# Three partial products for r in the steps of a two-layer token mixer, and its first score mask moved to other engines

## The chip, the cores and the metric

One core of one Trainium2 chip runs the whole kernel. TensorE (PE) multiplies, VectorE (DVE), ScalarE (ACT) and GpSimd (POOL) do the element-wise work, and SyncE (SP) issues the loads and stores. The metric is the device time of one execution in microseconds, taken over several executions.

## The reference

The input x is 4 sequences of 1024 tokens with 256 channels, float32. Two residual layers follow each other.

```python
# layer 1, on a = layernorm(x)
q = a @ Wq + bq
k = (a @ Wk + bk) @ Wc @ We          # 64 columns: 4 heads of 16
v = (a @ Wv + bv) @ Wc @ We
qf, kf = elu(q) + 1, elu(k) + 1      # 16 query heads share 4 key heads
o = (qf . cumsum(kf v)) / (qf . cumsum(kf) + 1e-6)
x = x + layernorm(a + o @ Wo + bo) * gamma + beta
# layer 2, on z = layernorm(x)
xr = mu_r * z + (1 - mu_r) * z_prev  # z_prev: the token before
xk = mu_k * z + (1 - mu_k) * z_prev
r = sigmoid(xr @ W_r.T)
out = x + r * (square(relu(xk @ W_k.T)) @ W_v.T)
```

## The kernel before

The tokens are worked in 8 chunks of 128 tokens, all 4 sequences (batches b) at once, so a chunk is a tile of 128x1024. `step(c)` of each engine runs for c = 0 to 6 and then `finale(7)`. The order of every engine's work is written out by hand in its `step`; semaphores tie the engines together, and each engine does its own list strictly in order.

Step c works on three chunks at once: n = c+1 (its queries, keys and values), c (its attention), m = c-1 (output projection, residual, first layernorm) and f = c-2 (the second layer, called the FFN here). Steps 2 to 6 have an FFN (f >= 0); these five are the repeating part. The FFN of the last three chunks is in the finale.

What the change touches, with the lines of the profile:

- Scores. PE writes the scores of one batch into the four banks `ps_z` (L471). DVE's `mask(c, b)` multiplies them with `causal` into `probs[b % 2]` (L1086), and PE's `outputs(c, b)` (L487, L492) reads these. `mask(c, 0)` is the first thing in DVE's step. PE's `spread_reciprocals` (L454) writes `ps_z` again and so waits for that mask; ACT copies its result out as `rden_bc`.
- Second layer. PE transposes z (`transpose_z`, L508), ACT copies it to `zT` (`shift_z`), after moving one column (128x8) as carry. POOL's `token_difference` makes `dz` in two halves (L290). DVE's `token_shift` (L1145) makes `xr` (two halves, early in the step) and `xk` (two halves, later), each from `dz` and `zT`. PE's `mix_r` (L522) multiplies xr with W_r in float32, 8 products of 128x256, each issued as two matmuls. `mix_k` (L515) and `mix_v_parts` (L553, L557) follow.
- Products in parts. For the queries and for v, ACT copies a float32 tile to type fp32r (the high part), DVE subtracts to get the low part, and PE makes three products: high x high, high x low, low x high. `low_a` (L1203) and `low_part` (L1209) are the DVE sides. `mix_r_parts` (L532, L536) does this for r in the finale, for the last chunk only.
- Norms. POOL's `first_norm(m)` (L225, L227) turns the variance of y into `rstd1`, which DVE's `second_residual` (`x2_tok`, listed as x_tok, L1130) needs. `norm_x(n+1)` does it for x. POOL's `add_bo` (`abo_tok`, L267) and `add_beta` (`xb_tok`, L274) are 128x1024 adds, `denominator_terms` (`prod`, L282) a 128x1024 product.
- Key features. ACT makes exp(k) (L801), DVE clips it at 1 (L1041) and makes kf (L1044). DVE's `centre` (y_tok, L1119) lies between `keys_values` (L1036, L1037) and that.
- Each list waits where it must; DVE's list in an FFN step is: mask 0, norm_x, xr (2), add_residual 0 and 1 with their statistics, mask 1, keys_values, centre (4), key_features, low_a (2), second_residual (4), divide 0, mask 2, queries 0, xk (2), queries 1, divide 1, states, key_sums, second_stats, mask 3, divide 2, low_part (2), reciprocal, divide 3, gate (2).

Of the kernel before, what the change touches and what calls it, by code (L numbers as in the profile page):

```python
# [7 lines left out]
P = 128  # L8
# [10 lines left out]
def build(nc, x, wq, bq, wk, bk, wv, bv, wc, we, wo, bo, gamma, beta, w_r, w_k, w_v, mu_r, mu_k, out):  # L19
# [14 lines left out]
    with ExitStack() as ctx:  # L34
# [16 lines left out]
        def view(t, start, *shape):  # L51
# [41 lines left out]
        prod = sb("prod", 2, T)  # L93
# [13 lines left out]
        xr_p, wr_split, s_xrh, s_xrl = aT_p, sem("wr_split"), sem("xr_high"), sem("xr_low")  # L107
        s_aTh, s_aTl, wq_split = sem("aT_high"), sem("aT_low"), sem("wq_split")
        s_kah, s_kal, wv_split = sem("kact_high"), sem("kact_low"), sem("wv_split")
        y_tok, z_tok = sb("y_tok", NB, D), sb("z_tok", NB, D)  # L110
# [24 lines left out]
        s_kv_ps, s_kv, s_ek, s_ekm, s_kf, s_vh, s_vp = (  # L135
            sem("kv_ps"), sem("kv_ready"), sem("expk"), sem("expk_min"), sem("kf_ready"), sem("v_half_ready"), sem("v_heads_ready"))
# [10 lines left out]
        s_vl, s_gl = sem("last_v_ps"), sem("last_gated")  # L147
        s_last, s_den = sem("last_out_ready"), sem("den_ready")
# [21 lines left out]
            16 * len(part) for part in (kv_loads, c_loads, bias_loads, q_loads, ffn_loads, row_loads))  # L170
        ka_value = lambda m: 2 * m + 2 if m < LAST else 2 * (LAST - 2) + 2
# [43 lines left out]
        def _(pool):  # L215
# [83 lines left out]

            def step(c):  # L300
                n, m, f = c + 1, c - 1, c - 2
                if f >= 0:
                    token_difference(f)
                if n + 1 < NC:
                    norm_x(n + 1)
                if f >= 0:
                    add_bo(n)
                    first_norm(m)
# [79 lines left out]
        def _(pe):  # L388
# [137 lines left out]
            def mix_r_parts(i, bk_):  # L526
                pe.wait_ge(s_xrh, 2)
                for b in (2 * i, 2 * i + 1):
# [4 lines left out]
                    if b == 0:  # L533
                        pe.wait_ge(s_xrl, 2)
# [44 lines left out]
            def step(c):  # L579
# [90 lines left out]
            def finale(c):  # L670
# [114 lines left out]
        def _(act):  # L785
# [11 lines left out]
            def keys(n):  # L797
# [3 lines left out]
                AC.activation(ek[:], kb[:], ACT.Exp).then_inc(s_ek, 1)  # L801
# [89 lines left out]

            def gate_r(m, i, bk_):
# [4 lines left out]

            def step(c):
                n, m, f = c + 1, c - 1, c - 2
                if f >= 0:  # L900
                    shift_z(f, x0, x1)
# [9 lines left out]
                if f >= 0:  # L911
                    for k in range(KD):
# [35 lines left out]
            def finale(c):  # L948
# [60 lines left out]
        def _(dve):  # L1009
# [151 lines left out]
            def step(c):  # L1161
                n, m, f = c + 1, c - 1, c - 2
                mask(c, 0)
# [9 lines left out]
                add_residual(m, 0, x1)  # L1173
                add_residual(m, 1, x2)
# [62 lines left out]
            def finale(c):  # L1237
# [34 lines left out]
                for k in range(KD):  # L1272
                    dve.wait_ge(s_xrh, k + 1)
                    V.tensor_tensor(xr_p[1][:, k, :], xr[:, k].rearrange("p b t -> p (b t)"), xr_p[0][:, k, :].bitcast(F32),
                                    ALU.subtract).then_inc(s_xrl, 1)
# [78 lines left out]
```

## Time and profile before

| | |
|---|---|
| median of 3 executions | 276.59 us (276.57 to 277.20) |
| the profiled execution | 276.82 us, span 275.1 us, so 1.7 us lie around the span |
| granted TensorE clock, mean | 0.984 |
| PE | 258.8 us busy, 94% |
| DVE | 229.4 us busy, 83% |
| ACT | 163.8 us busy, 60% |
| POOL | 143.9 us busy, 52% |

A line of the timeline has a start in us from the beginning of the span, a duration, the engine, the line of the kernel, out<-in, shapes and a count; neighbours of one kind are merged, so that the duration of "x2" covers both. Brackets hold the idle time before it and what ended it. POOL's busy time includes time in which it waits for memory.

### The profile page before, as it was taken

What the parts mean: (1) busy time and instruction counts of PE and PEld (TensorE: products, weight loads), DVE (VectorE), ACT (ScalarE), POOL (GpSimd) and SP (SyncE); (2) the same over time, 40 slices, a digit from 0 to 9 for tenths busy, and PEclk for the clock granted to TensorE, in tenths of its full rate; (3) what the DMA queues carried; (4) which work ended last, traced back from release to release, by engine and by line L of the source; (5) the groups of instructions that cost most, each with busy time, mean ns of one, the idle gap of its engine ahead of it and who ended that gap; (6) DMA issues with size and microseconds to landing.
All of it is one profiled execution on the core that took longest, in us unless ns stands there. A gap on an engine that the chain in (4) does not pass through costs nothing.

```text
span 275.1 us, 7641 instructions
## 1 busy us (share of the span) xinstructions
PE 258.8 (94%) x2997; PEld 193.6 (70%) x2997; DVE 229.4 (83%) x558; ACT 163.8 (60%) x329; POOL 143.9 (52%) x165
## 2 busy tenths in 40 slices
PE   7998989987999999999999999999999999997993
PEld 6856557745787588758886688758875777683863
DVE  6578576875999989898999989996999868999484
ACT  1458585675756965486737964686348830363680
POOL 2636494599653678335833686355533633055340
PEclk9799999997999999999999999999999999999998
DMA  5910220000200021000400020001000020000213
GB/s 156 287 61 1 79 77 6 4 0 2 76 4 2 0 93 64 1 4 13 142 2 2 2 76 4 1 4 47 32 2 4 2 76 2 2 0 0 77 38 118
DMA packets 12180, 10.75 MB, mean 39 GB/s; under 512 B 2288, under 2 KB 12144, under 8 KB 12144
## 3 DMA queue, kind: packets, MB, share of 16 engines
q1 hardware_dynamic: 11392, 9.97, 11.3%
q8 instruction: 24, 0.39, 0.6%
q10 hardware_dynamic: 752, 0.30, 0.4%
q14 instruction: 12, 0.10, 0.1%
HBM read 6.07 MB, written 4.19 MB: 37 GB/s over the span
## 4 chain that ended last, share of the span: by engine, by line
PE 57%; DVE 17%; issue 9%; ACT 7%; POOL 6%; DMA 2%; POOLq 1%; DVEq 0%; ACTq 0%
PE ps_x L500 9%; PE ps_x L515 7%; PE ps_x L522 6%; PE ps_x L404 4%; PE ps_z L471 4%; PE ps_y L487 4%; PE ps_y L492 4%; PE ps_x L553 4%; DVE xk L1145 4%; DVE stats L1014 2%; PE ps_z L731 2%; DMA out_dram<-out_tok 2%; PE ps_x L397 2%; PE ps_x L417 2%; PE ps_x L508 2%
## 5 line engine op out<-in xcount | busy, mean ns | idle before, releaser
L1086 DVE TENSOR_TENSOR probs<-ps_z,causal 128x1024 f32<-128x1024 f32 x32 | 38.7, 1208 | 1.0 <-PE ps_z L471 0.8
L274 POOL TENSOR_TENSOR xb_tok<-x_in,beta_bc 128x1024 f32<-128x1024 f32 x8 | 19.1, 2388 | 22.0 <-DVE x_tok L1130 22.0
L500 PE MATMUL ps_x<-wo_sb,oT 128*128 128x256 f32 x128 | 29.9, 382 | 0.0
L297 POOL TENSOR_TENSOR out_tok<-tanh_r,x_tok 128x512 f32<-128x512 f32 x14 | 18.3, 1313 | 20.9 <-DVE tanh_r L1158 20.9
L282 POOL TENSOR_TENSOR prod<-qf,ksum 128x1024 f32<-128x1024 f32 x7 | 16.5, 2359 | 22.3 <-DVE ksum L1059 22.3
L267 POOL TENSOR_TENSOR abo_tok<-a_tok,bo_bc 128x1024 f32<-128x1024 f32 x8 | 18.9, 2365 | 17.0 <-issue 6.8
L500 PEld LDWEIGHTS ps_x<-wo_sb,oT 128*128 128x128 f32 x128 | 23.5, 190 | 3.7 <-issue 0.5
L227 POOL TENSOR_TENSOR rstd<-rstd,neg_half 128x4 f32<-128x4 f32 x24 | 24.5, 1021 | 1.9
L487 PE MATMUL ps_y<-qf,state 32*32 32x128 f32 x512 | 20.9, 278 | 3.9 <-DVE oT L1098 3.4
L471 PE MATMUL ps_z<-qf,kfT 32*128 32x128 f32 x512 | 23.5, 298 | 0.9 <-DVE qf L1050 0.4
L487 PEld LDWEIGHTS ps_y<-qf,state 32*32 32x32 f32 x512 | 12.2, 105 | 16.0 <-issue 13.1
L471 PEld LDWEIGHTS ps_z<-qf,kfT 32*128 32x128 f32 x512 | 17.4, 187 | 6.9 <-issue 4.5
L492 PE MATMUL ps_y<-probs,v_pad 128*32 128x128 f32 x512 | 21.1, 283 | 0.0
L290 POOL TENSOR_TENSOR dz<-zT 128x512 f32<-128x512 f32 x14 | 14.7, 1073 | 8.2 <-ACT zT L789 8.2
L515 PE MATMUL ps_x<-xk,wkT 128*128 128x512 f32 x40 | 18.5, 605 | 0.4
L809 ACT ACTIVATE eq<-ps_x,neg_bq 128x512 f32<-128x512 f32 x15 | 10.3, 687 | 13.6 <-PE ps_x L420 12.8
L522 PE MATMUL ps_x<-wrT,xr 128*128 128x256 f32 x80 | 18.1, 379 | 0.0
L789 ACT ACTIVATE zT<-ps_x 128x512 f32<-128x512 f32 x16 | 8.7, 594 | 15.7 <-PE ps_x L508 15.7
L855 ACT ACTIVATE a_tok<-x_in,nbias,rstd 128x256 f32<-128x256 f32 x24 | 12.4, 589 | 8.8 <-issue 5.5
L869 ACT ACTIVATE z_tok<-x_tok,nbias,rstd 128x256 f32<-128x256 f32 x32 | 16.6, 594 | 0.6 <-POOL nbias L235 0.6
L1050 DVE SCALAR_TENSOR_TENSOR qf<-ps_x,bq,eq 128x512 f32<-128x512 f32 x15 | 11.2, 748 | 6.8 <-ACT eq L811 6.8
L492 PEld LDWEIGHTS ps_y<-probs,v_pad 128*32 128x32 f32 x512 | 12.2, 110 | 6.6 <-issue 6.1
(175 smaller groups left out, 663.4 us busy)
## 6 DMA issues: line engine op xcount, KB each, us to landing
x_in<-in_L_attn_x_dram SPq DMA_DIRECT2D x8, 512.0 KB, 4.3
out_dram<-out_tok SPq DMA_DIRECT2D x16, 256.0 KB, 2.1
xr<-in_L_attn_Wq_dram ACTq DMA_DIRECT2D x1, 256.0 KB, 4.2
xk<-in_L_ffn_W_r_dram SPq DMA_DIRECT2D x1, 256.0 KB, 5.5
xk<-in_L_ffn_W_k_dram SPq DMA_DIRECT2D x1, 256.0 KB, 5.7
xr<-in_L_ffn_W_v_dram SPq DMA_DIRECT2D x1, 256.0 KB, 6.3
wo_sb<-in_L_attn_Wo_dram SPq DMA_DIRECT2D x4, 64.0 KB, 4.6
bo_bc<-in_L_attn_bo_dram SPq DMA_DIRECT2D x1, 128.0 KB, 5.5
```

Source lines behind the costliest of these rows:

```text
L227: PL.tensor_tensor(dst[:], dst[:], neg_half[:], ALU.pow).then_inc(done, 1)
L267: PL.tensor_tensor(abo_tok[n % 2][:], a_tok[n % 2][:], bo_bc[:].unsqueeze(1).to_broadcast([P, NB, D]), ALU.add).then_inc(s_ab, 1)
L274: PL.tensor_tensor(xb_tok[n % 2][:], x_in[n % XBUF][:], beta_bc[:].unsqueeze(1).to_broadcast([P, NB, D]), ALU.add).then_inc(s_xb, 1)
L297: PL.tensor_tensor(out_tok[:, 2 * i:2 * i + 2, :], tanh_r[:, i].rearrange("p (b d) -> p b d", b=2), x2_tok[m % 3][:, 2 * i:2 * i + 2, :], ...
L471: last = mm(ps_z[:, g, u * P:(u + 1) * P], kfT[c % 2][rows, 2 * b + u, :, :], qf[c % 2][rows, :, t0:t0 + HALF], start=True, stop=True, ski ...
L487: mm(ps_y[rows, off + u * P:off + (u + 1) * P], state[rows, slot, b, :, :], qf[c % 2][rows, :, t0:t0 + HALF], start=(u == 0), stop=False, ...
L492: last = mm(ps_y[32 * g:32 * g + 32, off + u * P:off + (u + 1) * P], v_pad[c % 2][:, b, u, g, :, :], probs[b % 2][:, g, u * P:(u + 1) * P] ...
L500: last = mm(bk_[:, (b % 2) * D:(b % 2 + 1) * D], oT[m % 2][:, a, b, :], wo_sb[:, a, :], start=(a == 0), stop=(a == 1))
L515: last = mm(bk_[:, :], wkT[:, k, n * P:(n + 1) * P], xk[:, k, :, :], start=(k == 0), stop=(k == KD - 1))
L522: last = mm(bk_[:, (b % 2) * D:(b % 2 + 1) * D], xr[:, k, b, :], wrT[:, k, :], start=(k == 0), stop=(k == KD - 1))
L869: AC.activation(z_tok[:, b, :], x2_tok[m % 3][:, b, :], ACT.Identity, bias=nbias2[:, b:b + 1], scale=rstd2[:, b:b + 1]).then_inc(s_z, 1)
L1086: V.tensor_tensor(probs[b % 2][:].rearrange("p g (r s) -> p g r s", s=HALF), ps_z[:, :, 0:2 * P].rearrange("p g (r s) -> p g r s", s=HALF) ...
```

## The change

1. r of the FFN steps is made in three products of parts. ACT gets `high_xr(f)` (two copies of 128x512), DVE gets `low_xr(f)` (two subtractions of 128x512) between the two `add_residual`, PE runs `mix_r_parts` in place of `mix_r`. The parts of xr get tiles of their own; the space comes from `prod` (now the same tile as `eq`) and `z_tok` (now `a_tok`).
2. `mask(c, 0)` of the FFN steps leaves DVE. ACT copies the first scores to `probs[0]` (`first_scores`, ahead of `shift_z`), POOL multiplies them in place with `causal` (`mask_first`, between `token_difference` and `norm_x`), and `outputs(c, 0)` waits for POOL.
3. The clip of exp(k) leaves DVE: ACT computes relu(-k) and then exp of its negative, two instructions in place of one.
4. DVE's order becomes queries 0, xk 0, queries 1, xk 1.
5. POOL does `first_norm(m)` ahead of `add_bo(n)`.
6. Waits that go with the shared tiles: ACT's queries wait for the denominators of the chunk before, `normalise_z` for `add_bo`.

```diff
-        prod = sb("prod", 2, T)
+        prod = eq
...
-        xr_p, wr_split, s_xrh, s_xrl = aT_p, sem("wr_split"), sem("xr_high"), sem("xr_low")
+        xr_p = [ctx.enter_context(nc.sbuf_tensor(f"xr_{part}", [P, KD, T], F32R)) for part in ("high", "low")]
...
-        y_tok, z_tok = sb("y_tok", NB, D), sb("z_tok", NB, D)
+        y_tok, z_tok = sb("y_tok", NB, D), a_tok
...
+            def mask_first(c):
+                pool.wait_ge(s_pr, 8 * c + 2)
+                rows = probs[0][:].rearrange("p g (r s) -> p g r s", s=HALF)
+                PL.tensor_tensor(rows, rows, causal[:].unsqueeze(1).unsqueeze(1).to_broadcast([P, G, 4, HALF]),
+                                 ALU.mult).then_inc(s_first, 1)
...
                 if f >= 0:
                     token_difference(f)
+                if f >= 0:
+                    mask_first(c)
                 if n + 1 < NC:
                     norm_x(n + 1)
                 if f >= 0:
+                    first_norm(m)
                     add_bo(n)
-                    first_norm(m)
                     add_beta(n)
...
             def outputs(c, b):
+                if b == 0 and 2 <= c < LAST:
+                    pe.wait_ge(s_first, c - 1)
...
                     pe.wait_ge(s_y, 2 * m + 1)
-                    mix_r(f, 0, x1)
+                    pe.wait_ge(wr_split, 2)
+                    mix_r_parts(f, 0, x1)
                     pe.wait_ge(s_y, 2 * m + 2)
-                    mix_r(f, 1, x2)
+                    mix_r_parts(f, 1, x2)
...
-                AC.activation(ek[:], kb[:], ACT.Exp).then_inc(s_ek, 1)
+                AC.activation(ek[:], kb[:], ACT.Relu, scale=-1.0).then_inc(s_nk, 1)
+                act.wait_ge(s_nk, n + 1)
+                AC.activation(ek[:], ek[:], ACT.Exp, scale=-1.0).then_inc(s_ek, 1)
...
+            def high_xr(m):
+                if m >= 1:
+                    act.wait_ge(s_r_ps, 2 * m)
+                for k in range(KD):
+                    act.wait_ge(s_xr, 2 * m + k + 1)
+                    copy(xr_p[0][:, k, :], xr[:, k].rearrange("p b t -> p (b t)")).then_inc(s_xrh, 1)
...
+            def first_scores(c):
+                act.wait_ge(s_sc, 8 * c + 2)
+                act.wait_ge(s_o, 4 * c - 1)
+                copy(probs[0][:], ps_z[:, :, 0:2 * P]).then_inc(s_pr, 2)
+
             def step(c):
                 n, m, f = c + 1, c - 1, c - 2
                 if f >= 0:
+                    first_scores(c)
                     shift_z(f, x0, x1)
...
                 if f >= 0:
+                    high_xr(f)
                     for k in range(KD):
                         act.wait_ge(s_aT, 2 * n + k + 1)
...
             def key_features(n):
                 dve.wait_ge(s_ek, n + 1)
-                V.tensor_scalar(ek[:], ek[:], 1.0, None, ALU.min).then_inc(s_ekm, 1)
-                dve.wait_ge(s_ekm, n + 1)
...
-                mask(c, 0)
+                if f < 0:
+                    mask(c, 0)
...
                 add_residual(m, 0, x1)
+                low_xr(f)
                 add_residual(m, 1, x2)
...
                 queries(n, 0, x0)
                 token_shift(f, 0, *for_k)
+                queries(n, 1, x1)
                 token_shift(f, 1, *for_k)
-                queries(n, 1, x1)
...
+            def low_xr(m):
+                if m >= 1:
+                    dve.wait_ge(s_r_ps, 2 * m)
+                for k in range(KD):
+                    dve.wait_ge(s_xrh, xr_value(m) - 1 + k)
+                    V.tensor_tensor(xr_p[1][:, k, :], xr[:, k].rearrange("p b t -> p (b t)"), xr_p[0][:, k, :].bitcast(F32),
+                                    ALU.subtract).then_inc(s_xrl, 1)
```

## Rows read from the trace of the kernel before

**Rows 1.** Busy time of each engine in one whole FFN step (step 4).

```profile
core 0: us, PE busy (x) PEld busy (x) DVE busy (x) ACT busy (x) POOL busy (x), PEclk, DMA share, GB/s
128.73:159.00 30.27, 30.07 (x370) 22.81 (x369) 28.04 (x68) 20.43 (x41) 17.43 (x18) 1.00 0.12 36
```

**Rows 2.** Timeline of PE in the same step.

```profile
138.18 3.62 PE L522 MATMUL ps_x<-wrT,xr 128*128 128x256 f32 x16
...
155.93 0.39 PE L553 MATMUL ps_x<-wv_high,ka_high 128*128 128x256 f32 x1
...
159.00 0.73 PE L471 MATMUL ps_z<-qf,kfT 32*128 32x128 f32 x16
```

**Rows 3.** Timeline of DVE in the same step.

```profile
132.52 1.87 DVE L1145 SCALAR_TENSOR_TENSOR xr<-dz,mu_r_col,zT 128x512 f32<-128x512 f32 x2
...
137.55 1.19 DVE L1086 TENSOR_TENSOR probs<-ps_z,causal 128x1024 f32<-128x1024 f32 x1
...
139.32 1.66 DVE L1119 SCALAR_TENSOR_TENSOR y_tok<-y_tok,mv,gamma_bc 128x256 f32<-128x256 f32 x4
140.90 0.29 DVE L1041 TENSOR_SCALAR ek<-ek 128x256 f32<-128x256 f32 x1
141.30 0.43 DVE L1044 SCALAR_TENSOR_TENSOR kf<-kb,ek 128x256 f32<-128x256 f32 x1
141.65 1.28 DVE L1203 TENSOR_TENSOR aT_low<-aT,aT_high 128x512 fp32r<-128x512 f32 x2
...
144.76 1.22 DVE L1086 TENSOR_TENSOR probs<-ps_z,causal 128x1024 f32<-128x1024 f32 x1
146.61 0.75 DVE L1050 SCALAR_TENSOR_TENSOR qf<-ps_x,bq,eq 128x512 f32<-128x512 f32 x1 [0.63 <-ACT eq L811]
...
153.00 1.19 DVE L1086 TENSOR_TENSOR probs<-ps_z,causal 128x1024 f32<-128x1024 f32 x1
154.31 0.42 DVE L1098 TENSOR_TENSOR oT<-ps_y,rden_bc 128x256 f32<-128x256 f32 x1
```

**Rows 4.** Timeline of ACT in the same step.

```profile
130.47 1.09 ACT L789 ACTIVATE zT<-ps_x 128x512 f32<-128x512 f32 x2 [2.36 <-PE ps_x L508]
...
131.92 1.04 ACT L789 ACTIVATE rden_bc<-ps_z 128x1024 f32<-128x1024 f32 x1
...
158.17 0.21 ACT L789 ACTIVATE zT<-zT 128x8 f32<-128x8 f32 x1
```

**Rows 5.** Timeline of POOL in the same step.

```profile
131.14 2.04 POOL L290 TENSOR_TENSOR dz<-zT 128x512 f32<-128x512 f32 x2 [0.18 <-ACT zT L789]
...
136.57 2.37 POOL L267 TENSOR_TENSOR abo_tok<-a_tok,bo_bc 128x1024 f32<-128x1024 f32 x1 [0.74 <-ACT a_tok L855]
138.90 0.20 POOL L225 TENSOR_TENSOR rstd<-mv,ln_eps 128x4 f32<-128x4 f32 x1
139.18 1.02 POOL L227 TENSOR_TENSOR rstd<-rstd,neg_half 128x4 f32<-128x4 f32 x1
144.59 2.41 POOL L274 TENSOR_TENSOR xb_tok<-x_in,beta_bc 128x1024 f32<-128x1024 f32 x1 [4.39 <-DVE x_tok L1130]
```

**Rows 6.** Timeline of DVE and POOL at two moments of the finale, one instruction a line.

```profile
246.32 0.48 DVE L1130 SCALAR_TENSOR_TENSOR x_tok<-y_tok,rstd,xb_tok 128x256 f32<-128x256 f32 x1
246.40 1.30 POOL L290 TENSOR_TENSOR dz<-zT 128x512 f32<-128x512 f32 x1 [1.11 <-ACT zT L789]
...
246.72 1.26 DVE L1130 SCALAR_TENSOR_TENSOR x_tok<-y_tok,rstd,xb_tok 128x256 f32<-128x256 f32 x1
...
247.66 1.22 POOL L290 TENSOR_TENSOR dz<-zT 128x512 f32<-128x512 f32 x1
247.90 1.52 DVE L1145 SCALAR_TENSOR_TENSOR xk<-dz,mu_k_col,zT 128x512 f32<-128x512 f32 x1
```

**Rows 7.** Busy time and granted clock in two stretches of step 1.

```profile
61.20:64.60 3.40, 1.21 (x32) 0.78 (x32) 3.31 (x8) 2.56 (x7) 3.24 (x6) 1.00 0.00 0
64.60:68.10 3.50, 3.44 (x56) 2.61 (x60) 0.40 (x2) 1.83 (x5) 3.50 (x2) 0.51 0.02 5
```

More of the change, by code:

```diff
@@ L106, in build @@
         wr_p = [ctx.enter_context(nc.sbuf_tensor(f"wr_{part}", [P, KD, D], F32R)) for part in ("high", "low")]
-        xr_p, wr_split, s_xrh, s_xrl = aT_p, sem("wr_split"), sem("xr_high"), sem("xr_low")
+        xr_p = [ctx.enter_context(nc.sbuf_tensor(f"xr_{part}", [P, KD, T], F32R)) for part in ("high", "low")]
+        wr_split, s_xrh, s_xrl = sem("wr_split"), sem("xr_high"), sem("xr_low")
         s_aTh, s_aTl, wq_split = sem("aT_high"), sem("aT_low"), sem("wq_split")
         s_kah, s_kal, wv_split = sem("kact_high"), sem("kact_low"), sem("wv_split")
-        y_tok, z_tok = sb("y_tok", NB, D), sb("z_tok", NB, D)
+        y_tok, z_tok = sb("y_tok", NB, D), a_tok
         stats1, mv1, rstd1 = sb("stats1", NB, 6), sb("mv1", NB, 2), sb("rstd1", NB)
@@ L134, in build @@
             sem("aT_ps"), sem("aT_ready"), sem("q_ps"), sem("negq"), sem("expq"), sem("qf_ready"))
-        s_kv_ps, s_kv, s_ek, s_ekm, s_kf, s_vh, s_vp = (
-            sem("kv_ps"), sem("kv_ready"), sem("expk"), sem("expk_min"), sem("kf_ready"), sem("v_half_ready"), sem("v_heads_ready"))
+        s_kv_ps, s_kv, s_ek, s_nk, s_kf, s_vh, s_vp = (
+            sem("kv_ps"), sem("kv_ready"), sem("expk"), sem("negk"), sem("kf_ready"), sem("v_half_ready"), sem("v_heads_ready"))
         s_kT_ps, s_kT, s_ks, s_dS_ps, s_tail, s_state = (
@@ L147, in build @@
         s_vl, s_gl = sem("last_v_ps"), sem("last_gated")
+        s_first = sem("first_probs_masked")
         s_last, s_den = sem("last_out_ready"), sem("den_ready")
@@ L170, in build @@
             16 * len(part) for part in (kv_loads, c_loads, bias_loads, q_loads, ffn_loads, row_loads))
+        xr_value = lambda m: 2 * m + 2 if m < LAST else 2 * (LAST - 2) + 2
         ka_value = lambda m: 2 * m + 2 if m < LAST else 2 * (LAST - 2) + 2
@@ L507, in transpose_z @@
                     for k, bk_ in ((0, bk0), (1, bk1)):
-                        last = tr(bk_[:, b * P:(b + 1) * P], z_tok[:, b, k * P:(k + 1) * P], ident[:])
+                        last = tr(bk_[:, b * P:(b + 1) * P], z_tok[m % 2][:, b, k * P:(k + 1) * P], ident[:])
                         if b == NB - 1:
@@ L524, in mix_r, with mix_r_parts @@
                 last.then_inc(s_r_ps, 1)
-            def mix_r_parts(i, bk_):
-                pe.wait_ge(s_xrh, 2)
+            def mix_r_parts(m, i, bk_):
+                pe.wait_ge(s_xrh, xr_value(m))
                 for b in (2 * i, 2 * i + 1):
@@ L533, in mix_r_parts @@
                     if b == 0:
-                        pe.wait_ge(s_xrl, 2)
+                        pe.wait_ge(s_xrl, xr_value(m))
                     for k in range(KD):
@@ L720, in finale @@
                 pe.wait_ge(wr_split, 2)
-                mix_r_parts(0, z2)
+                mix_r_parts(c, 0, z2)
                 pe.wait_ge(s_th, 2 * m + 2)
-                mix_r_parts(1, z3)
+                mix_r_parts(c, 1, z3)
                 pe.wait_ge(s_gt, 2 * m + 1)
@@ L808, in queries @@
                     act.wait_ge(s_qf, 2 * n - 1 + a)
+                    act.wait_ge(s_den_ps, n)
                 AC.activation(eq[:, a, :], bk_[:, :], ACT.Relu, bias=neg_bq[:, a:a + 1], scale=-1.0).then_inc(s_nq, 1)
@@ L865, in normalise_z @@
                 act.wait_ge(s_nb2, 2 * m + 2)
+                act.wait_ge(s_ab, min(m + 3, NC))
                 if m >= 1:
@@ L868, in normalise_z @@
                 for b in range(NB):
-                    AC.activation(z_tok[:, b, :], x2_tok[m % 3][:, b, :], ACT.Identity, bias=nbias2[:, b:b + 1],
+                    AC.activation(z_tok[m % 2][:, b, :], x2_tok[m % 3][:, b, :], ACT.Identity, bias=nbias2[:, b:b + 1],
                                   scale=rstd2[:, b:b + 1]).then_inc(s_z, 1)
@@ L963, in finale @@
                 gate_r(m, 1, z3)
-                for k in range(KD):
-                    act.wait_ge(s_xr, 2 * c + k + 1)
-                    copy(xr_p[0][:, k, :], xr[:, k].rearrange("p b t -> p (b t)")).then_inc(s_xrh, 1)
+                high_xr(c)
                 channel_k(c, 0, z0, True)
@@ L1271, in finale @@
                 token_shift(c, 1, *for_r)
[L1272 to L1275, printed above, removed]
+                low_xr(c)
                 gate(m, 0, x1)
```

## The prediction

> **What bounds it now.** I read the page's busy shares first, then the chain that ended last, then cut the span into steps. The chain repeats five times with a period of 30.27 us, and most of it is PE; in one such step PE is busy for 30.07 of 30.27 us at full clock, and DVE for 28.04 [rows 1]. So PE sets the pace, but DVE is nearly full and has almost no air. To see how much, I followed DVE's list through one step. It waits in only two kinds of place. One is 0.63 us ahead of queries 0, for ACT's exponential [rows 3]. The other is where PE has to deliver: divide 2 starts at 154.31, while a mask that starts at 153.00 leaves DVE free about 1.14 us later (144.76 plus 1.22, less the 0.08 by which neighbours overlap), at 154.14, so 0.17 us of slack; and the two gates at the step's end, which wait for mix_v and are PE's business. Between xr at the front and divide 2 the list therefore has 0.8 us of air, and divide 2 releases PE's last outputs, mix_v and with them the next step. Whatever lengthens DVE by more than 0.8 us in that stretch lengthens the step.
>
> I call T the start of the scores that open a step, 128.73 here (159.00 less the period) [rows 1, 2].
>
> **What decides: who blocks whom.** In the finale DVE runs four x_tok in a row, each 0.48 us. POOL's dz is issued at 246.40, while the third runs. The fourth, issued at 246.72, takes 1.26 us in place of 0.48 and ends at 247.98, 0.28 behind dz's end at 247.70; dz itself takes 1.30 [rows 6], of which 1.02 is its own time by the pair of 2.04 [rows 5]. Then xk, issued at 247.90 under the second dz (which ends at 248.88), takes 1.52 and ends 0.54 behind it [rows 6]. So a POOL instruction and a DVE instruction of two SBUF inputs exclude each other for their whole length, and a waiting POOL instruction gets in between two DVE instructions that stand back to back. The masks, which read PSUM, are not stretched: 1.19 with abo_tok running over it, 1.22 with xb_tok [rows 3, 5]. In the step the same is seen at xr: two halves take 1.87 us, since the first waits for the second dz [rows 3, 5].
>
> The Trainium skill (SBUF — State Buffer, section "SBUF: two separate sides") states this as a rule: VectorE and GpSimd share one pair of ports, a VectorE instruction with two SBUF inputs and a GpSimd one that reads SBUF take it as an exclusive lock for the whole instruction, and the other "fully blocks". By that rule the sum is the one below; were the two to share the ports in parts, or not at all, it would be the fourth case. The trace agrees, by the 1.26 and 1.52 us above.
>
> **The change part by part**, on DVE's path from zT to divide 2, in us per FFN step.
>
> 1. First scores on ACT. They end at about T+0.73 [rows 2]. The copy is bound by rden_bc, the same shape out of the same banks: 1.04 us; the carry column (0.21, now done ahead of the step in idle time) comes behind it [rows 4]. zT then starts at T+1.95 in place of T+1.74 (130.47) [rows 4]. That is +0.21 for dz. DVE itself is freed of 1.14 us ahead of norm_x, and this is worth nothing: DVE then stands waiting for dz, which hangs on PE's transposes and ACT.
> 2. mask_first on POOL. Its price is that of abo_tok, 128x1024 with a broadcast, 2.37 us; xb_tok at 2.41 bounds it above and the two dz halves at 2.04 below [rows 5]. It is issued when the second dz ends, while xr 0 has been waiting for the ports; xr 0 goes first, as now; mask_first waits and goes in between, as dz did between the x_tok; xr 1 is blocked. It begins some 0.12 ahead of xr 0's end (246.80 against 247.70 less 1.02 [rows 6]), and xr 1 ends 0.54 behind it in place of 0.66 behind xr 0: 2.37 - 0.12 + 0.54 - 0.66 = +2.13. The wait that outputs 0 gets for it costs nothing: the mask ends near T+7.5, outputs 0 comes after T+13.
> 3. low_xr on DVE, the same as aT_low: 1.28 less 0.08 overlap [rows 3], +1.20. Its high parts are ready: ACT needs about 0.55 us behind each xr (half of zT's 1.09 [rows 4]), and add_residual 0 with its statistics stands between.
> 4. first_norm ahead of add_bo. Today abo_tok runs from 136.57 to 138.94, under statistics, mask 1 and keys_values, and ends before centre at 139.32 [rows 3, 5]. In the new order POOL waits for the statistics of y, which end where mask 1 starts (call it 0), does L225 and L227 (0.07 + 0.28 + 1.02, less 0.04) and begins abo_tok at 1.33, until 3.70. Centre is issued at 139.32 - 137.55 = 1.77 and has two SBUF inputs. Its first instruction ends at 3.98 and not at 2.25: +1.73. The other order would have avoided this only if POOL were free early, which mask_first and the norm of x behind it prevent.
> 5. The clip goes: 140.90 to 141.30 [rows 3], -0.40. ACT's second instruction on the keys (kf of the same size takes 0.43 on DVE, so about 0.45) is covered by centre's 1.66 [rows 3].
> 6. k's shifts. xb_tok starts behind x_tok, 0.17 ahead of mask 2, and ends at 147.00. Without the 0.63 us of air, queries 0 would start at 145.90 and xk 0 at 146.57; it waits until 147.00 and ends 0.54 later, 147.54 in place of 147.31 [rows 3, 5]: +0.23. That queries 1 comes one shift earlier lets mix_k start some 0.66 earlier against DVE, but the end of the stretch is divide 2, and DVE's sum up to there is unchanged: 0.
> 7. r in parts. mix_r takes 3.62 less overlap, 3.54; the same count of products in parts takes 155.93 to 159.00, 3.07 [rows 2]. PE is shorter by 0.47, and this is worth nothing here, since PE will wait for DVE.
> 8. ACT gets 1.04 + 1.09 + 0.45 = 2.6 us on 20.4 of 30.27 [rows 1, 4]: covered. The waits for the shared tiles look at work of the step before: 0. Steps 0 and 1 and the finale change by a tenth at most.
>
> **Sum:** 0.21 + 2.13 + 1.20 + 1.73 - 0.40 + 0.23 = 5.10; less the air, 0.63 and 0.17: **+4.30 us a step**, a period of 34.6 us. Five steps: +21.5. Against the profiled execution (276.82, which is 0.23 above the median of the runs) that gives **298.3 us**. With mask_first between 2.04 and 2.41 it is 296.7 to 298.5.
>
> **Rivals.**
>
> - *The clock falls.* Low_a ends near T+19.1 (141.65 + 1.28 is T+14.2 today [rows 3], and items 1 to 5 add 4.87), and PE, with its high products done, would be there near T+16: a wait of about 3 us. In step 1 PE was busy for 1.21 of 3.40 us and the granted clock was then 0.51, the lower of the two levels (1.2 GHz in place of 2.4), for 3.5 us [rows 7]. Such a fall costs up to half of 3.5 us, of which part lies in the wait. From 0 to 1.75 a step, I take 0.8: 302.3 us. For it: the wait is longer than any in an FFN step now. Against it: before and behind it PE is dense. Chance 0.15.
> - *xr 1 gets the ports ahead of mask_first.* Then mask_first runs from the end of xr 1, and low_xr, issued 1.4 us later, waits about 0.85 for it. In place of 2.13 the step pays 0.85: +3.0 a step, 291.9 us. Against it stands x_tok and dz. Chance 0.12.
> - *Only one of the two large blocks happens*, since abo_tok or mask_first comes at another time than I place it: 4.30 - 1.73 = 2.57 or 4.30 - 2.13 = 2.17 a step, 289.7 or 287.7 us. Chance 0.10.
> - *The blocks do not count*, as if the ports were free: 0.21 + 1.20 - 0.40 - 0.80 = +0.21, or nothing at all if xr 1 runs unblocked. 276.6 to 277.9 us. Chance 0.06.
> - *Faster.* DVE's list is a little shorter by count (1.14 and 0.40 go, 1.20 comes), and PE loses 0.47 us. If the step stays PE's, as it is by the shares, all of that shows: 5 x 0.47 = 2.4 us, 274.4 us. Its place is mix_r on PE; it decides if what DVE gets up to divide 2 stays under its 0.8 us of air, so if mask_first and abo_tok both fall under instructions that read PSUM. Chance 0.07.
>
> The forecast has 0.50. The range is 287 to 304: it takes in the first three rivals and leaves out the last two with 0.13 and the tails. A measurement of this kernel tells apart about 0.3%, 0.8 us. Slower by over that has 0.50 + 0.15 + 0.12 + 0.10 and part of the fourth, 0.89; within it 0.04; faster 0.07.
>
> **What will show it.** In an FFN step of the new profile: one of the two xr takes near 3 us with mask_first over it; the first centre takes about 2.2 us in place of 0.48, with abo_tok over it; PE is idle for several us, ended by DVE's aT_low and xr_low; the period is about 34.6 us; mix_r_parts takes 3.1 us. I am wrong if mask_first and xr run over each other unstretched, if the centre instructions stay at 0.48, or if PE stays busy for 29.5 us of a shorter step.

## The result and the profile after

The changed kernel takes 300.75 us (median of 4, 299.32 to 302.62) beside 276.89 us for the kernel before (median of 4, 276.57 to 277.54): a ratio of 1.0876, 95% interval 1.0839 to 1.0914. The forecast was 298.3 us, range 287 to 304. The profiled execution took 300.64 us, its span 298.9.

The page of the changed kernel, parts 1 and 2, to be read against the table of the kernel before:

```profile
PE 263.8 (88%) x3037; PEld 196.0 (66%) x3037; DVE 249.0 (83%) x555; ACT 177.6 (59%) x352; POOL 156.4 (52%) x170
...
PEclk9999999979999999799998999779997999999999
```

PE fell from 94% to 88% of a longer span, and DVE's busy time rose by 19.6 us although three fewer instructions run on it: its instructions are longer, not more. The clock row shows four dips in the repeating steps that were not there before (at 122, 156, 191 and 228 us); the one near 65 us, in step 1, is in both pages.

Three FFN steps of the changed kernel, busy time by engine (columns as in [rows 1]):

```profile
101.78:136.91 35.13, 31.37 (x381) 23.46 (x380) 32.03 (x68) 22.99 (x45) 19.91 (x19) 0.95 0.11 32
136.91:172.07 35.16, 31.43 (x380) 23.71 (x380) 32.13 (x68) 23.00 (x45) 20.07 (x19) 0.95 0.10 31
172.07:208.43 36.36, 32.60 (x380) 24.42 (x380) 32.26 (x68) 22.99 (x45) 19.66 (x19) 0.91 0.05 16
```

The period was 30.27 us. DVE has 68 instructions in a step as before, and 32.1 us busy in place of 28.0. T, the start of the scores, is 136.84 for the second of these. DVE's timeline in that step:

```profile
140.69 4.20 DVE L1173 SCALAR_TENSOR_TENSOR xr<-dz,mu_r_col,zT 128x512 f32<-128x512 f32 x2 [1.25 <-POOL dz L293]
144.82 0.68 DVE L1137 TENSOR_TENSOR y_tok<-ps_x,abo_tok 128x512 f32<-128x512 f32 x1
...
146.20 1.28 DVE L1240 TENSOR_TENSOR xr_low<-xr,xr_high 128x512 fp32r<-128x512 f32 x2
...
149.20 1.19 DVE L1114 TENSOR_TENSOR probs<-ps_z,causal 128x1024 f32<-128x1024 f32 x1
...
150.97 3.50 DVE L1147 SCALAR_TENSOR_TENSOR y_tok<-y_tok,mv,gamma_bc 128x256 f32<-128x256 f32 x4
...
157.85 1.21 DVE L1114 TENSOR_TENSOR probs<-ps_z,causal 128x1024 f32<-128x1024 f32 x1
...
159.64 0.96 DVE L1173 SCALAR_TENSOR_TENSOR xk<-dz,mu_k_col,zT 128x512 f32<-128x512 f32 x1
160.99 0.75 DVE L1078 SCALAR_TENSOR_TENSOR qf<-ps_x,bq,eq 128x512 f32<-128x512 f32 x1 [0.40 <-ACT eq L828]
...
166.06 1.19 DVE L1114 TENSOR_TENSOR probs<-ps_z,causal 128x1024 f32<-128x1024 f32 x1
167.31 0.42 DVE L1126 TENSOR_TENSOR oT<-ps_y,rden_bc 128x256 f32<-128x256 f32 x1
```

and POOL's:

```profile
139.54 2.04 POOL L293 TENSOR_TENSOR dz<-zT 128x512 f32<-128x512 f32 x2 [0.46 <-ACT zT L803]
141.54 2.81 POOL L306 TENSOR_TENSOR probs<-probs,causal 128x1024 f32<-128x1024 f32 x1
...
150.62 2.38 POOL L270 TENSOR_TENSOR abo_tok<-a_tok,bo_bc 128x1024 f32<-128x1024 f32 x1
157.67 2.38 POOL L277 TENSOR_TENSOR xb_tok<-x_in,beta_bc 128x1024 f32<-128x1024 f32 x1 [4.67 <-DVE x_tok L1158]
```

Two of DVE's instructions by themselves, the second xr and the first centre:

```profile
142.05 2.84 DVE L1173 SCALAR_TENSOR_TENSOR xr<-dz,mu_r_col,zT 128x512 f32<-128x512 f32 x1
...
150.97 2.31 DVE L1147 SCALAR_TENSOR_TENSOR y_tok<-y_tok,mv,gamma_bc 128x256 f32<-128x256 f32 x1
```

The reader is to lay the two engines on each other. Mask_first is issued at 141.54, waits for xr 0, and takes 2.81 us, of which about 2.37 are its own (the price of abo_tok). The second xr is issued at 142.05 and ends at 144.89: 2.84 us in place of 0.74. Abo_tok starts at 150.62, 0.35 ahead of centre, whose four instructions then take 3.50 us in place of 1.66, all of the excess in the first (2.31). Xb_tok holds xk back by 0.2. Mask 2 at 157.85 reads PSUM; xb_tok runs over all of it, and it takes 1.21 us, as before (1.22). DVE is idle for 1.25 us ahead of xr, which is the place where mask 0 used to be.

PE waits for aT_low, and in four of the five FFN steps the clock falls behind the wait. PE's timeline of the step, and its busy time and clock before and behind:

```profile
156.05 0.96 PE L431 MATMUL ps_x<-aT_low,wq_high 128*128 128x512 f32 x2 [2.94 <-DVE aT_low L1233]
156.81 0.63 PE L428 MATMUL ps_x<-aT_high,wq_high 128*128 128x512 f32 x1
```

```profile
153.10:156.50 3.40, 0.46 (x3) 0.40 (x3) 3.40 (x9) 0.90 (x2) 0.00 (x0) 0.98 0.00 0
156.50:160.00 3.50, 3.50 (x24) 2.36 (x22) 3.50 (x7) 1.71 (x3) 2.33 (x1) 0.53 0.00 0
...
190.70:197.50 6.80, 6.27 (x43) 4.20 (x44) 6.14 (x11) 3.89 (x8) 2.39 (x1) 0.51 0.01 2
```

With 0.46 us of work in 3.40, the granted clock is then 0.53, the lower level (1.2 GHz), for 3.5 us; in the following step it stays there for 6.8 us, and that step is the one of 36.36 us. The first FFN step has the same wait and no fall:

```profile
86.41 0.50 PE L431 MATMUL ps_x<-aT_low,wq_high 128*128 128x512 f32 x1 [2.96 <-DVE aT_low L1233]
...
86.40:89.90 3.50, 3.49 (x43) 2.48 (x44) 3.50 (x7) 2.63 (x5) 1.88 (x1) 1.00 0.00 0
```

### The profile page after: what moved, and what is told of

Same layout as the page of the kernel before. It is cut to its first block, busy times and chain, and to the rows that moved or that the text cites. A ratio compares the mean times of both kernels' runs of the same rounds, so it can differ in the third digit from the quotient of the medians.

```text
span 298.9 us, 7762 instructions
## 1 busy us (share of the span) xinstructions
PE 263.8 (88%) x3037; PEld 196.0 (66%) x3037; DVE 249.0 (83%) x555; ACT 177.6 (59%) x352; POOL 156.4 (52%) x170
## 4 chain that ended last, share of the span: by engine, by line
PE 46%; DVE 33%; issue 9%; ACT 6%; POOL 4%; DVEq 0%; POOLq 0%; ACTq 0%
PE ps_x L513 5%; DVE xr L1173 5%; PE ps_x L528 5%; DVE stats L1044 4%; PE ps_y L500 4%; DVE y_tok L1147 4%; PE ps_y L505 4%; PE ps_x L566 4%; DVE probs L1114 3%; PE ps_z L482 3%; DVE y_tok L1137 3%; PE ps_x L431 2%; PE ps_x L521 2%; DVE aT_low L1233 2%; PE ps_x L428 2%
## 5 line engine op out<-in xcount | busy, mean ns | idle before, releaser
L1114 DVE TENSOR_TENSOR probs<-ps_z,causal 128x1024 f32<-128x1024 f32 x27 | 32.5, 1203 | 0.9 <-PE ps_z L482 0.8
L1173 DVE SCALAR_TENSOR_TENSOR xr<-dz,mu_r_col,zT 128x512 f32<-128x512 f32 x16 | 25.2, 1617 | 7.5 <-POOL dz L293 7.5
L285 POOL TENSOR_TENSOR eq<-qf,ksum 128x1024 f32<-128x1024 f32 x7 | 16.6, 2368 | 21.7 <-DVE ksum L1087 21.7
L500 PE MATMUL ps_y<-qf,state 32*32 32x128 f32 x512 | 22.0, 290 | 4.2 <-DVE oT L1126 3.8
L431 PE MATMUL ps_x<-aT_low,wq_high 128*128 128x512 f32 x20 | 9.3, 558 | 14.8 <-DVE aT_low L1233 14.8
L505 PE MATMUL ps_y<-probs,v_pad 128*32 128x128 f32 x512 | 21.9, 292 | 0.0
L1147 DVE SCALAR_TENSOR_TENSOR y_tok<-y_tok,mv,gamma_bc 128x256 f32<-128x256 f32 x28 | 20.9, 803 | 0.0
L887 ACT ACTIVATE a_tok<-x_tok,nbias,rstd 128x256 f32<-128x256 f32 x32 | 16.6, 592 | 0.7 <-POOL nbias L238 0.6
L415 PE MATMUL ps_x<-wkv_sb,aT 128*128 128x128 f32 x128 | 16.4, 282 | 0.5 <-ACT aT L803 0.5
L234 POOL TENSOR_TENSOR neg_mean<-mv,neg_one 128x4 f32<-128x4 f32 x17 | 5.6, 327 | 21.3 <-DVE mv L1050 21.2
```

The source lines that it names most:

```text
L1114: V.tensor_tensor(probs[b % 2][:].rearrange("p g (r s) -> p g r s", s=HALF), ps_z[:, :, 0:2 * P].rearrange("p g (r s) -> p g r s", s=HALF) ...
L1147: V.scalar_tensor_tensor(out=y_tok[:, b, :], in0=y_tok[:, b, :], scalar=mv1[:, b, 0:1], in1=gamma_bc[:], op0=ALU.subtract, op1=ALU.mult).t ...
L1173: V.scalar_tensor_tensor(out=dst[:, k], in0=dz[:, k], scalar=mu[:, k:k + 1], in1=zT[:, k, :, 0:P], op0=ALU.mult, op1=ALU.add).then_inc(don ...
```

## The experiments

All ratios are against the kernel before on the same chip. The medians in us come from more than one chip, so where two variants are compared the ratios are the safer pair. A step's period is read from the starts of the second gate (DVE tanh_r) in two successive steps, unless another row is shown.

**1. Is the clock fall a cost of its own?** The high products of queries 0 are issued three times more, in PE's wait.

```diff
             def query_parts(n, a, bk_):
                 pe.wait_ge(s_aTh, 2 * n - 4)
+                for again in range(3 if a == 0 else 0):
+                    for k in range(KD):
+                        for part in range(2):
+                            mm(bk_[:, :], wq_p[part][:, k, a, :], aT_p[0][:, k, :], start=(k == 0 and part == 0),
+                               stop=(k == 1 and part == 1))
```

> The changed kernel, with the four high products of queries 0 issued three times more ahead of the real ones: 12 x 0.23 = 2.8 us of PE work inside the 2.94 us that PE waits for aT_low in each FFN step. Theory (the wait costs a clock fall on top of DVE's chain): the granted clock stays at the upper level in the FFN steps, aT_low's products and queries 1 take 0.4 to 0.63 us each no more, DVE no longer waits for queries 1; the step goes from 35.1 to 36.4 us to 34.6 to 34.9 us, the kernel to 297.0 to 298.5 us. Rival (the fall lies wholly inside time in which PE would wait anyway): 300.7 us as the changed kernel, within 0.5.

Measured: 298.25 us (297.56 to 298.81), ratio 1.0803 (1.0760 to 1.0846). Two of its steps, and PE behind the wait:

```profile
102.58:137.12 34.54, 32.89 (x392) 25.01 (x392) 31.96 (x68) 23.00 (x45) 19.91 (x19) 1.00 0.11 32
137.12:171.65 34.53, 32.88 (x392) 24.99 (x392) 31.95 (x68) 22.99 (x45) 19.89 (x19) 1.00 0.10 32
```

```profile
121.74 0.73 PE L436 MATMUL ps_x<-aT_low,wq_high 128*128 128x512 f32 x2 [0.23 <-DVE aT_low L1238]
```

The clock stays at the upper level (1.00) and the step is 34.53 us: 12 needless products in each FFN step make the kernel faster, by 2.5 us in the medians, 2.0 by the two ratios and 2.9 between the spans of the profiled executions (298.9 and 296.0). This is also the forecast's own case without the fall, and the period stands against its 34.57 (30.27 + 4.30). The rest, 0.6 us in three steps and 1.8 in one, is the clock: 3.7 us in all. The span gives back 0.8 less than that, because this execution has a longer stretch at the lower level in step 1: its first FFN step ends 0.8 us later (second gate at 102.69 in place of 101.89).

**2. POOL's order.** Part 5 undone: add_bo ahead of first_norm.

```diff
-                    first_norm(m)
                     add_bo(n)
+                    first_norm(m)
                     add_beta(n)
```

> The changed kernel with POOL's add_bo ahead of first_norm again (part 5 undone). Theory: in the changed kernel POOL is free at T+10.1 and y's second half is there at T+11.2, so add_bo runs from T+11.3 to T+13.7 under statistics, mask 1 and keys_values, and ends before centre at T+14.1. Centre takes 1.66 in place of 3.50 us, and PE's wait for aT_low falls from 2.9 to about 1.1 us, which brings no clock fall: 1.84 a step and the falls' 3 us: 288.5 to 292 us. Rival (the prediction's own item 4: POOL is too late for this order because of mask_first and norm_x, and abo_tok blocks centre anyway): 299 to 301 us.

Measured: 288.54 us (288.14 to 288.94), ratio 1.0452 (1.0412 to 1.0492); period 32.68. Timeline of step 3, POOL, DVE and PE:

```profile
111.06 2.40 POOL L270 TENSOR_TENSOR abo_tok<-a_tok,bo_bc 128x1024 f32<-128x1024 f32 x1 [1.29 <-ACT a_tok L872]
113.81 1.66 DVE L1147 SCALAR_TENSOR_TENSOR y_tok<-y_tok,mv,gamma_bc 128x256 f32<-128x256 f32 x4
...
117.06 0.73 PE L431 MATMUL ps_x<-aT_low,wq_high 128*128 128x512 f32 x2 [1.11 <-DVE aT_low L1233]
```

Abo_tok now ends at 113.46, 0.35 ahead of centre, and centre takes 1.66. One pair of swapped lines is worth 12 us. The step is 1.85 us shorter than in experiment 1, which is centre's 1.84. The clock falls in the FFN steps are gone as well, with PE's wait down to 1.11 us; the profiled execution has one in the finale instead (two gates there stand 12.17 us apart in place of 10.73). The prediction had said that the old order could not help; it is refuted.

**3. Mask 0 back on DVE**, part 2 undone, POOL's new order kept.

```diff
-                if f >= 0:
-                    mask_first(c)
...
-                    first_scores(c)
...
-                if f < 0:
-                    mask(c, 0)
+                mask(c, 0)
```

> The changed kernel with mask 0 on DVE again, without first_scores and mask_first (part 2 undone), POOL's new order kept. Theory (ports): mask 0 fills the time in which DVE waits for dz, so it costs nothing; xr takes 1.87 us again in place of 4.20, dz comes 0.2 earlier; centre stays blocked by abo_tok (3.5 us). Per step 1.20 + 1.84 - 0.40 + 0.23 - 0.80 = +2.1 over the kernel before: 285.5 to 288 us. Rival (mask 0 on DVE costs its 1.14 us, and taking it off is a gain that the rest hides): 291 to 294 us.

Measured: 286.67 us (286.60 to 287.75), ratio 1.0394 (1.0352 to 1.0436); period 32.13, which is +1.86 on the kernel before and -2.4 on experiment 1. POOL and DVE in step 3:

```profile
103.23 1.87 DVE L1168 SCALAR_TENSOR_TENSOR xr<-dz,mu_r_col,zT 128x512 f32<-128x512 f32 x2
...
110.82 2.38 POOL L270 TENSOR_TENSOR abo_tok<-a_tok,bo_bc 128x1024 f32<-128x1024 f32 x1
111.17 3.50 DVE L1142 SCALAR_TENSOR_TENSOR y_tok<-y_tok,mv,gamma_bc 128x256 f32<-128x256 f32 x4
```

Xr has its old 1.87 us and centre is blocked as before, so the two blocks are separate. Giving DVE a 1.2 us instruction back makes the step 2.4 us shorter than it is without it.

**4. Both undone**: left are r in parts, the clip on ACT, the order at k's shifts, and the shared tiles with their waits.

> Parts 2 and 5 both undone: left are r in parts, the clip on ACT, the order at k's shifts. Theory: DVE's list up to divide 2 has 1.20 more and 0.40 less, against 0.80 of air, and up to 0.23 from xb_tok over xk: 0 to +0.25 a step, so 276.3 to 278.3 us, and PE's shorter r brings nothing. Rival (r in parts pays as PE's sum says): 5 x 0.47 less, 274.0 to 275.0 us.

Measured: 277.70 us (275.93 to 279.59), ratio 1.0048 (1.0012 to 1.0084); period 30.29 in the step shown, 30.48 in another. DVE's timeline:

```profile
131.56 1.87 DVE L1168 SCALAR_TENSOR_TENSOR xr<-dz,mu_r_col,zT 128x512 f32<-128x512 f32 x2
...
139.51 1.66 DVE L1142 SCALAR_TENSOR_TENSOR y_tok<-y_tok,mv,gamma_bc 128x256 f32<-128x256 f32 x4
...
152.28 1.19 DVE L1109 TENSOR_TENSOR probs<-ps_z,causal 128x1024 f32<-128x1024 f32 x1
153.39 0.41 DVE L1121 TENSOR_TENSOR oT<-ps_y,rden_bc 128x256 f32<-128x256 f32 x1
```

Xr and centre have their old lengths. Divide 2 starts 1.11 behind mask 3, back to back, where it stood 1.31 behind in the kernel before [rows 3]: DVE's air is used up, and r in parts gives nothing. The profiled execution is the fastest of ten; over all ten the kernel is half a per cent slower than the kernel before, clear of noise. The shared tiles and their waits (part 6) were not run alone, but they are in this kernel too, so 0.2 us a step bounds them unless r in parts saves what they cost.

**5. Where mask_first stands in POOL's queue.** Mask_first ahead of token_difference.

```diff
                 if f >= 0:
-                    token_difference(f)
+                    mask_first(c)
                 if f >= 0:
-                    mask_first(c)
+                    token_difference(f)
```

> The changed kernel with POOL's mask_first ahead of token_difference. Theory (POOL's 2.4 us and dz are in one queue ahead of xr, so the order makes little difference): the mask runs from T+2.2 to T+4.6 under norm_x's statistics, dz from T+4.6 to T+6.6, xr ends at T+7.8 in place of T+8.0; xr's two halves take about 1.9 us again, but DVE waits some 3 us for dz: 0.2 a step less, 298.5 to 300.5 us. Rival (the loss is only the port that mask_first takes between the two xr): 288 to 291 us.

Measured: 299.64 us (298.12 to 300.50), ratio 1.0837 (1.0790 to 1.0885), which its interval does not tell apart from the changed kernel's 1.0876; the rival, 288 to 291 us, is out. POOL and DVE in one step:

```profile
138.96 2.35 POOL L306 TENSOR_TENSOR probs<-probs,causal 128x1024 f32<-128x1024 f32 x1
141.27 2.03 POOL L293 TENSOR_TENSOR dz<-zT 128x512 f32<-128x512 f32 x2
```

```profile
142.42 2.10 DVE L1173 SCALAR_TENSOR_TENSOR xr<-dz,mu_r_col,zT 128x512 f32<-128x512 f32 x2 [3.06 <-POOL dz L293]
```

The block of xr is gone (2.10 us), and the wait for dz has grown to 3.06. The 2.4 us on POOL stand in series with DVE's path at either place, once through the ports and once through the queue. So "the port is the loss" would be a wrong lesson on its own: a place is wanted where POOL's work is ahead of nothing that DVE needs and over nothing of two SBUF inputs.

**6. Does it take a read to block?** Mask_first becomes five memsets of half of probs[0]. ACT still copies the first scores out, but the memsets overwrite them, so the kernel leaves out batch 0's scores in the FFN steps: that tile is zero.

```diff
-                rows = probs[0][:].rearrange("p g (r s) -> p g r s", s=HALF)
-                PL.tensor_tensor(rows, rows, causal[:].unsqueeze(1).unsqueeze(1).to_broadcast([P, G, 4, HALF]),
-                                 ALU.mult).then_inc(s_first, 1)
+                for i in range(5):
+                    last = PL.memset(probs[0][:, 2 * (i % 2):2 * (i % 2) + 2, :], 0.0)
+                    if i < 4:
+                        link(last)
+                last.then_inc(s_first, 1)
```

> The changed kernel with mask_first replaced by five memsets of half of probs[0], of about the same total time, which read nothing (the first scores of the FFN steps are left out: that tile is zero). Theory (only a GpSimd instruction that reads SBUF excludes a DVE instruction of two SBUF inputs): xr's two halves take 1.9 us in place of 4.2, the step loses 2.1 us and PE's wait for aT_low falls to about 1 us, with no clock fall: 286 to 289.5 us. Rival (any GpSimd instruction on SBUF blocks): 296 to 301 us.

Measured: 289.27 us (286.62 to 290.39), ratio 1.0457 (1.0407 to 1.0507). DVE and POOL in one step:

```profile
137.09 2.10 DVE L1175 SCALAR_TENSOR_TENSOR xr<-dz,mu_r_col,zT 128x512 f32<-128x512 f32 x2 [1.25 <-POOL dz L293]
```

```profile
137.92 2.85 POOL L306 MEMSET probs<- 128x512 f32 x5
```

The memsets run over the whole of the second xr, and the two xr take 2.10 us and not 4.20, the same as in experiment 5, where no 128x1024 instruction of POOL's runs over the second. A write alone does not exclude DVE, as the Trainium skill (SBUF — State Buffer, section "SBUF: two separate sides") has it. One step of this kernel kept the upper clock:

```profile
166.48:198.90 32.42, 29.88 (x380) 22.65 (x383) 29.86 (x69) 22.86 (x45) 19.56 (x23) 1.00 0.06 18
```

It is 2.1 us shorter than the step of experiment 1, which is item 2 of the prediction (2.13), and 0.3 longer than that of experiment 3, which is what ACT's copy of the scores ahead of zT costs. Three of the four executions show a mean clock of 0.97 and take 288.9 to 290.4 us, one shows 0.988 and takes 286.6: against what was expected, the clock falls had not gone altogether. Centre is still blocked by abo_tok, so PE's wait is 1.81 us and not the 1 us expected, and behind it the clock fell in three of four steps. Behind the waits of experiments 2 (1.11) and 3 (1.23 to 1.60) it fell in none.

**7. The clip and the order at k's shifts alone**, on the kernel before.

```diff
-                AC.activation(ek[:], kb[:], ACT.Exp).then_inc(s_ek, 1)
+                AC.activation(ek[:], kb[:], ACT.Relu, scale=-1.0).then_inc(s_ekm, 1)
+                act.wait_ge(s_ekm, n + 1)
+                AC.activation(ek[:], ek[:], ACT.Exp, scale=-1.0).then_inc(s_ek, 1)
...
-                V.tensor_scalar(ek[:], ek[:], 1.0, None, ALU.min).then_inc(s_ekm, 1)
-                dve.wait_ge(s_ekm, n + 1)
...
-                token_shift(f, 1, *for_k)
                 queries(n, 1, x1)
+                token_shift(f, 1, *for_k)
```

> The kernel before with the clip of exp(k) on ACT and DVE's new order at k's shifts, nothing else. Theory: the 0.40 us of the clip only lengthens the wait for ACT's exponential from 0.63 to about 1.0 us (0); queries 1 comes 0.66 earlier, mix_k starts without its 0.14 us of wait: 0.1 to 0.2 a step, 0.5 to 1.0 us less than the kernel before on the same chip. Rival (DVE's time counts wherever it is taken off): 5 x 0.4 and more, at least 2 us less.

Measured: 276.66 us (275.16 to 277.28), ratio 1.0009 (0.9986 to 1.0033): as a time, no difference. In the trace the period is 30.14 (gates at 128.58 and 158.72), 0.13 less than before, as expected; five times that is below what the runs can tell. What is excluded is the rival, 2 us.

**8. A version that beats both.** R in parts, clip and order stay. Mask 0 is DVE's. Mask 1 goes to ACT and POOL, where POOL has a gap and DVE reads PSUM; add_bo waits for x_tok and add_beta goes to the end of the step.

```diff
             def mask_first(c):
-                pool.wait_ge(s_pr, 8 * c + 2)
-                rows = probs[0][:].rearrange("p g (r s) -> p g r s", s=HALF)
+                pool.wait_ge(s_pr, 8 * c + 4)
+                rows = probs[1][:].rearrange("p g (r s) -> p g r s", s=HALF)
...
                 if f >= 0:
                     token_difference(f)
-                if f >= 0:
-                    mask_first(c)
                 if n + 1 < NC:
                     norm_x(n + 1)
                 if f >= 0:
+                    mask_first(c)
                     first_norm(m)
+                    pool.wait_ge(s_x2, 4 * m + 4)
                     add_bo(n)
-                    add_beta(n)
                     denominator_terms(n)
                     second_norm(m)
+                    add_beta(n)
...
-                if b == 0 and 2 <= c < LAST:
+                if b == 1 and 2 <= c < LAST:
                     pe.wait_ge(s_first, c - 1)
...
             def first_scores(c):
-                act.wait_ge(s_sc, 8 * c + 2)
-                act.wait_ge(s_o, 4 * c - 1)
-                copy(probs[0][:], ps_z[:, :, 0:2 * P]).then_inc(s_pr, 2)
+                act.wait_ge(s_sc, 8 * c + 4)
+                act.wait_ge(s_o, 4 * c)
+                copy(probs[1][:], ps_z[:, :, 0:2 * P]).then_inc(s_pr, 2)
...
-                    first_scores(c)
                     shift_z(f, x0, x1)
...
                         copy(aT_p[0][:, k, :], aT[:, k, :]).then_inc(s_aTh, 1)
+                    first_scores(c)
...
-                if f < 0:
-                    mask(c, 0)
+                mask(c, 0)
...
                 add_residual(m, 1, x2)
-                mask(c, 1)
                 keys_values(n)
```

> Built from what the runs showed: r in parts, clip and order of the changed kernel, mask 0 on DVE, and in its place mask 1 copied out by ACT and masked by POOL, in a gap of POOL (T+8.7 to T+11.1) in which DVE runs instructions that read PSUM; add_bo waits for x_tok and takes the place of add_beta, which goes behind second_norm. Theory: DVE up to divide 2 has 1.20 - 1.11 - 0.40 and about 0.3 from centre's first instruction under the mask, so nothing more than before, and PE's 0.47 us shorter r shows, with 0.1 from the order: 0.4 to 0.6 a step, 2 to 3 us less than the kernel before on the same chip. Rival (mask 1 on POOL blocks centre longer, or ACT is late for aT and a_tok): 0 to 5 us more than the kernel before.

Measured: 272.92 us (272.79 to 274.82), ratio 0.9897 (0.9864 to 0.9930): 1% faster than the kernel before, clear of noise, and a little more than expected. Five steps of 0.61 us less make 3.0 of the 3.6 us. One step, and POOL and DVE in the next:

```profile
127.02:156.68 29.66, 29.58 (x380) 22.75 (x383) 28.29 (x69) 22.75 (x45) 19.90 (x19) 1.00 0.12 37
```

```profile
135.70 2.40 POOL L306 TENSOR_TENSOR probs<-probs,causal 128x1024 f32<-128x1024 f32 x1 [1.77 <-ACT probs L803]
```

```profile
137.44 2.14 DVE L1147 SCALAR_TENSOR_TENSOR y_tok<-y_tok,mv,gamma_bc 128x256 f32<-128x256 f32 x4
```

The same kind of mask on POOL at 2.40 us costs DVE 0.48 here (centre's 2.14 for 1.66), which is the part of it that is left when centre is issued. PE is busy for 29.58 of 29.66 us: it sets the pace again, with the shorter r.

**9. What of that is r?** Experiment 8 with r of the FFN steps in float32: `mix_r` in place of `mix_r_parts`, `high_xr(f)` and `low_xr(f)` taken out.

> The best version (mask 1 by ACT and POOL) with r of the FFN steps in float32 again, so without the two copies on ACT and the two subtractions on DVE. Theory: PE's r takes 3.54 us in place of 3.07, and since PE sets the pace once DVE has air, the step is 30.1 us in place of 29.66, as in the kernel with clip and order alone: 2.2 to 2.5 us above the best version, 275.0 to 276.3 us. Rival (the gain came from mask 1 leaving DVE, not from r): 271 to 273 us.

Measured: 276.65 us (275.58 to 278.52), ratio 1.0019 (0.9997 to 1.0041), a little above what was expected; the period is 30.10 (gates at 129.75 and 159.85), as expected. DVE has 1.2 us less to do than in experiment 8 and the kernel is 3.7 us slower (1.2% by the ratios). Of this, five steps of 0.44 us are 2.2; for the rest no run isolates the cause, but the clock takes part: the profiled execution here has a fall in the finale that experiment 8's has not, and the executions at a mean clock of 0.994 take 275.58 us here and 272.8 to 272.9 there. Moving the mask alone is worth nothing against clip and order alone (30.10 and 30.14, experiment 7), r in parts without it (experiment 4) is worth nothing; together, and with the 0.13 of clip and order, they are worth 0.6 us a step.

| kernel | us | ratio | period |
|---|---|---|---|
| before | 276.1 to 276.9 | 1 | 30.27 |
| changed | 300.75 | 1.0876 | 35.1 to 36.4 |
| 1: wait filled | 298.25 | 1.0803 | 34.53 |
| 5: mask first in POOL's queue | 299.64 | 1.0837 | 34.8 to 36.0 |
| 6: writes only | 289.27 | 1.0457 | 32.4 to 33.1 |
| 2: add_bo first | 288.54 | 1.0452 | 32.68 |
| 3: mask 0 on DVE | 286.67 | 1.0394 | 32.1 to 32.3 |
| 4: both | 277.70 | 1.0048 | 30.3 to 30.5 |
| 7: clip and order alone | 276.66 | 1.0009 | 30.14 |
| 8: mask 1 on POOL | 272.92 | 0.9897 | 29.66 |
| 9: the same, r in float32 | 276.65 | 1.0019 | 30.10 |

## Why the prediction was right, point by point

- **What bounds it, and DVE's air of 0.8 us.** Right, and this is what made the sum work. Experiment 4 adds 0.8 us net to DVE up to divide 2 and the period moves by 0.0 to 0.2.
- **Who blocks whom.** Right. Xr 1 took 2.84 us (said: near 3). The rival in which xr 1 gets the ports first is refuted by the same row.
- **Item 1**, +0.21 from ACT's copy: dz started at T+2.70 in place of T+2.41, so +0.3; experiments 3 and 6 differ by the same 0.3.
- **Item 2**, +2.13: xr ended at T+8.05 (144.89), expected T+8.00. With item 1 the block is 2.39 against the 2.34 of the sum; experiments 1 and 3 differ by 2.40.
- **Item 3**, +1.20: measured 1.20 (from xr_low at 146.20 to the next y_tok at 147.40).
- **Item 4**, +1.73: measured 1.84 (3.50 less 1.66). The size was right. The sentence behind it was wrong: "The other order would have avoided this only if POOL were free early, which mask_first and the norm of x behind it prevent." POOL was free at T+10.1, a microsecond before the second y_tok ends, for which add_bo waits; I had not put the two times beside each other. Experiment 2 shows 12 us for it.
- **Item 5 and item 6**: the clip left the list; xb_tok held xk for 0.22, said 0.23.
- **Item 7**: PE's shorter r brought nothing in the changed kernel; given room, it brings 0.44 a step (experiments 8 and 9), said 0.47.
- **Item 8**, "change by a tenth at most": the scores that open the first FFN step came 0.7 us earlier than in the kernel before. Most of it is there by 12 us already: the execution of the kernel before had a stretch at the lower clock in the second slice of its page (0.52 from 10.2 to 13.6 us), and this one has none there (1.00). I put it down to the clock; no run here isolates it. Executions of one and the same kernel differ in this way too: beside the experiments, those of the kernel before take 275.0 to 275.4 us at a mean clock of 0.989 to 0.994 and 276.1 to 277.2 at 0.984 to 0.988.
- **The sum**, 4.30 a step: 4.26 in experiment 1. What was missed is the clock. The forecast left it to a rival with a chance of 0.15 at 302.3 us, and that rival's case is the one that came, in four of five steps (122, 156, 191 and 228 us). The wait was foreseen (about 3 us, measured 2.94), and so was the price (0 to 1.75, taken as 0.8; measured 0.6, and 1.8 once), but not its likelihood. The argument against it was that PE is dense before and behind the wait; yet the row of step 1 had shown a fall behind a stretch with 1.21 us of work in 3.40 [rows 7], and this stretch was going to hold less.
- **How the total came about.** The profiled execution is 23.8 us above the profiled one of before (300.64 and 276.82). The first FFN step starts 0.7 us earlier and is 4.0 us longer (35.10 for 31.12 from the scores to the second gate; before, the end of a clock fall lay in it). The four periods behind it are 20.8 us longer, 17.1 by the sum and 3.7 by the clock falls, and the end is 0.2 shorter. Without the falls it would be 20.1 us, 1.4 below the forecast's 21.5. So the mechanism of the step was right to 0.04 us, while part of the closeness of the total is luck: what the opening and the first FFN step gave back hid over a third of the falls, and the median of 300.75 lies between the two cases, nearer to the rival's. It is in the range because the range took the rival in.

## What to carry to other kernels

Before work is handed from DVE to POOL, lay the new POOL instruction over DVE's list at the time at which it will run: in these traces it cost nothing over a mask that reads PSUM (1.21 us under xb_tok for 1.19 to 1.22 otherwise). In front of a DVE instruction of two SBUF inputs it cost what was left of it when that one was issued (2.1 of 2.4 us over xr, 1.84 over centre, 0.48 in experiment 8), and ahead of something that DVE waits for it cost about the same through the queue. An instruction that fills a wait of its engine costs nothing, so taking it off gains nothing. Where a change makes the matmul engine wait between dense stretches, look for what the granted clock did behind such stretches in the trace at hand, and put that case into the sum and not into a remote rival. Where two engines are both nearly full, a saving on one shows only with the matching room on the other; try the pair, not each alone.

## What was not expected of the hardware

Twelve products in each FFN step that compute nothing new made the kernel 2.0 to 2.5 us faster, by keeping the granted clock at 1.00 through a wait of 2.9 us. Waits of one length did not act alike: behind 2.94 to 2.96 us the clock fell in four of five steps, behind 1.81 in three of four. And a mask of 2.4 us cost 2.4 us a step at one place of POOL's list (2.1 by itself, 0.3 by ACT's copy for it) and 0.48 us of DVE's time at another, 4 us later in the step.
